# Outputs and maxima of an attention layer transposed on VectorE, outputs scaled on GpSimd, and a new order of the work

## The chip, the cores and the metric

The kernel runs on one core of a Trainium2 chip, as one launch. The metric is device time in microseconds (us), the median of three runs. The core's engines are TensorE (PE; PEld is its weight load), VectorE (DVE), ScalarE (ACT), GpSimd (POOL) and SyncE (SP), which here issues nearly all DMAs. Each engine works through its own instructions in order; semaphores tie them together.

## The reference

A layer over x of shape 4 x 1024 x 256 in float32: causal attention with 16 heads of 16 channels, a light feed-forward layer for all tokens, and a heavy one for 256 tokens of each batch, chosen by a router.

```python
xn = layernorm(x)
# attention; the reshape cuts the flat (token, channel) rows into 16 heads
qkv = (xn @ W_qkv + b_qkv).reshape(B, 16, S, -1)
q, k, v = split(qkv, 3, axis=-1)
qk = einsum('bhse,bhte->bhst', q, k) * 512 ** -0.5
attn = softmax(qk + causal_mask, axis=-1)
att = einsum('bhst,bhte->bhse', attn, v).reshape(B, S, -1) @ W_out + b_out
# feed-forward
light = gelu(rms_norm(xn, gamma_light) @ w1_light + b1_light) @ w2_light + b2_light
scores = coor_descent_route(xn, routing_token)      # 50 rounds of logsumexp
idx = top_k(scores, 256)
heavy = gelu(rms_norm(xn[idx], gamma_heavy) @ w1_heavy + b1_heavy) @ w2_heavy + b2_heavy
out = x + att + light + scatter(heavy, idx)
```

## The kernel before

**Front.** 32 tiles of 128 tokens are normalised, transposed on TensorE and projected to q, k, v and the routing score. VectorE adds the bias (`evacuate`, L1222) and SyncE stores each tile to DRAM (`qkv_d`, L612). Beside the last 16 tiles TensorE already does the transposes of q and k of the first steps and the maxima of step 0 (`FIRST`, `BESIDE`).

**Loop over 16 steps.** Step q holds four (batch, head) pairs, the "batches" c = 0 to 3. The work of a step:
- `T`: q and k are transposed (L968). ScalarE, VectorE (`R1`, L1244) and GpSimd (`SPLIT`, L1543, L1545) cut them into three bf16 pieces, which go through DRAM (`pieces_d`) into the operands `QTq` and `QTk`, rows 0 to 95. Operands have three buffers.
- `C`: 12 chunks of scores for each batch (L975), up to 512 columns wide, of which VectorE takes the row maxima only: L1256 where the chunk holds the diagonal (a custom instruction and one that reads its accumulator), L1259 where it doesn't. After chunk 11 of a batch a reduction gives the negated maxima `nm` (L1265).
- `MAX`: GpSimd cuts the maxima of one batch into three bf16 pieces (L1552 to L1557). `MT`: TensorE transposes them (L981), VectorE copies them (L1267), SyncE copies them into rows 96 to 98 of `QTq` (`load_m`, L658). They are subtracted inside the next matmul.
- `E`: 38 blocks of scores, keys on partitions (L1008), through two PSUM slots; ScalarE writes their exponentials to `strips` (L836). `CAUSAL`: GpSimd masks the diagonal (L1640).
- `PV`: 12 products with the values and a column of ones (L1026; four of 32 output rows side by side, two passes each, 8 matmul records), into `psO`.
- `OUT`: ScalarE copies the finished outputs to `osb` (L846). `OT`: TensorE transposes them in two halves (L987), and VectorE divides them by their sums (`normalise`, L1312 and L1317) into `pmo`. `SA`: one DMA stores them (L692).

`C` of a step runs about one step ahead of `E`. Router rounds (`R`, L1279, L1281, L1623) and a threshold search (`S`, L1286 to L1290) are mixed in. `T`, `C`, `MT` and `OT` share a ring of four PSUM slots (`MS`): TensorE waits until VectorE has freed the slot it needs (`free`). The order within each engine is made before the run by `schedule()`: it lets the engines advance in a model of costs (`TENSOR`, `VECTOR` and so on, `takes`), and picks, of what is ready, what is due first. The engines then run exactly this order. An item that isn't ready holds up all that stand behind it on its engine.

**After the loop** TensorE waits for the last output copy (`osb_done`) and does the light feed-forward layer (L1065) and the output projection in units; the last `OT` stands between the first two hidden products.

Two lines of `scores` and `product` matter for the waits:

```python
if kb == 0 and a == 0:
    pe.wait_ge(m_in[heads[0]], 16 * (q + 1))     # scores, one batch's maxima
...
if q > 0: pe.wait_ge(osb_done, q)                # product, kb == 0 and h == 0
```

## Time and profile before

| | us |
|---|---|
| median of three runs (792.14 to 795.06) | 793.27 |
| profiled execution | 791.96 |
| its span, first to last instruction | 790.2 |

| engine | busy us | share of the span |
|---|---|---|
| TensorE | 730.3 | 92% |
| VectorE | 576.0 | 73% |
| ScalarE | 435.3 | 55% |
| GpSimd | 366.9 | 46% |

Busy time is the time in which at least one instruction of the engine is under way. Matmuls are pipelined, so TensorE can be busy nearly all the time without being at its peak; the distance from one start to the next tells more than a duration. In the rows below `xN` is the number of instructions merged into a row, and "[t <-X]" says that the engine sat idle for t before the row, until X. The front takes some 130 us, the loop over steps 516, the rest 144.

### The profile page before, as it was taken

Reading aid. Unit: us, or ns where it says so; the run is one execution under the profiler, and the core shown is the slowest. Engines: PE = TensorE matmul, PEld = TensorE weight load, DVE = VectorE, ACT = ScalarE, POOL = GpSimd, SP = SyncE. Lnnn points to the kernel's source line nnn. Section 1 sums busy time; section 2 is a strip of 40 time slices with the busy share of each in tenths; the row PEclk is TensorE's granted clock in tenths of the full one; section 3 lists DMA queues with packets and bytes.
Section 4 is the critical chain, followed back from the end, with each engine's and each line's share of the span. In section 5 each row is a group of like instructions: output and inputs, shape, how many; then the busy total and the mean of one; then the engine's idle time right before and its main releaser. Section 6 shows DMA issues by size and latency. Waiting matters only on the chain.

```text
span 790.2 us, 13829 instructions
## 1 busy us (share of the span) xinstructions
PE 730.3 (92%) x4307; PEld 332.9 (42%) x4307; DVE 576.0 (73%) x1942; ACT 435.3 (55%) x940; POOL 366.9 (46%) x951
## 2 busy tenths in 40 slices
PE   5896998999899999999999999999999889978996
PEld 2563553333333333333333333333333238756655
DVE  4674776899899999999998999998998002554401
ACT  2232223577677777777777777767776661212240
POOL 5339102366565565755756556555332141235313
PEclk9999997799999999999999999999999999989999
DMA  9887854768989598678695795875902404652112
GB/s 286 212 203 164 210 160 111 150 120 96 194 116 102 113 98 125 116 76 147 98 108 108 90 140 103 88 129 62 129 7 29 121 7 131 197 174 93 11 17 27
DMA packets 246649, 92.18 MB, mean 117 GB/s; under 512 B 207504, under 2 KB 227120, under 8 KB 246576
## 3 DMA queue, kind: packets, MB, share of 16 engines
q1 hardware_dynamic: 245040, 89.20, 62.5%
q0 software_dynamic: 1536, 2.10, 1.7%
q8 instruction: 35, 0.57, 0.3%
q14 instruction: 38, 0.31, 0.2%
HBM read 56.26 MB, written 34.62 MB: 115 GB/s over the span
## 4 chain that ended last, share of the span: by engine, by line
PE 56%; DVE 29%; POOL 4%; issue 4%; ACT 3%; DMA 3%; SPq 1%; DVEq 0%; POOLq 0%
DVE ps L1256 12%; PE ps L1026 12%; PE ps L1008 10%; PE ps L975 9%; DVE mx L1259 8%; PE ps L943 7%; PE ps L1172 4%; PE ps L1185 3%; PE ps L1103 3%; ACT strips L836 2%; DVE mx L1256 2%; PE ps L1065 2%; PE ps L968 1%; PE ps L1099 1%; POOL roots L1499 1%
## 5 line engine op out<-in xcount | busy, mean ns | idle before, releaser
L836 ACT ACTIVATE strips<-ps 128x512 f32<-128x512 f32 (+1 forms) x608 | 325.9, 573 | 128.7 <-PE ps L1008 122.2
L1256 DVE CUSTOM_DVE_ANT_0 ps<-ps,maskrow 128x128 f32<-128x128 f32 (+3 forms) x512 | 244.7, 502 | 24.7 <-PE ps L975 23.9
L975 PE MATMUL ps<-QTk,QTq 96*128 96x512 bf16 (+3 forms) x768 | 212.9, 333 | 6.3 <-DVE mx L1256 2.7
L1008 PE MATMUL ps<-QTq,QTk 99*128 99x512 bf16 (+3 forms) x768 | 210.8, 334 | 7.3 <-ACT strips L836 4.2
L1259 DVE TENSOR_REDUCE mx<-ps 128x1 f32<-128x512 f32 x256 | 174.9, 683 | 16.2 <-PE ps L975 15.4
L1026 PE MATMUL ps<-strips,vext 128*32 128x512 f32 (+3 forms) x1536 | 165.0, 503 | 1.6 <-POOL strips L1640 1.1
L1008 PEld LDWEIGHTS ps<-QTq,QTk 99*128 99x128 bf16 x768 | 62.3, 97 | 142.3 <-ACT strips L836 115.8
L1640 POOL TENSOR_SCALAR_AFFINE_SELECT strips<-strips 128x512 f32<-128x512 f32 x128 | 80.4, 638 | 84.5 <-ACT strips L836 84.0
L975 PEld LDWEIGHTS ps<-QTk,QTq 96*128 96x128 bf16 x768 | 72.1, 98 | 112.3 <-DVE mx L1256 40.6
L943 PE MATMUL ps<-shared,xrT 128*128 128x384 f32 (+1 forms) x256 | 94.0, 502 | 1.2 <-DVE shared L1222 0.7
L1256 DVE DVE_READ_ACCUMULATOR2_ANT mx<- 128x1 f32 x512 | 71.6, 140 | 0.1
L943 PEld LDWEIGHTS ps<-shared,xrT 128*128 128x128 f32 x256 | 47.0, 195 | 30.7 <-issue 9.2
L1552 POOL CAST mW<-nm 128x8 bf16<-128x8 f32 x64 | 12.2, 190 | 100.6 <-DVE nm L1265 100.3
L1026 PEld LDWEIGHTS ps<-strips,vext 128*32 128x32 f32 x1536 | 30.7, 108 | 50.3 <-issue 39.8
L805 ACT ACTIVATE xrT<-ps 128x256 f32<-128x256 f32 x32 | 12.2, 380 | 54.8 <-PE ps L928 54.8
L1545 POOL TENSOR_TENSOR pieces<-r,pieces 128x512 bf16<-128x512 f32 x32 | 37.1, 1159 | 2.7
L1666 POOL TENSOR_TENSOR QTq<-QTq,shared 128x1024 f32<-128x1024 f32 x8 | 18.8, 2356 | 40.7 <-DMA QTq<-in_L_attn_inputs 40.6
L1392 DVE TENSOR_TENSOR QTk<-ps,QTq 128x256 f32<-128x256 f32 x32 | 13.4, 422 | 32.8 <-PE ps L1103 32.7
L791 ACT ACTIVATE xr<-strips,xshift,xscale 128x256 f32<-128x256 f32 x32 | 18.8, 592 | 28.8 <-POOLq L1515 28.8
L1103 PE MATMUL ps<-shared,strips 128*128 128x256 f32 x128 | 33.8, 388 | 0.0
L1312 DVE RECIPROCAL rden<-ps 128x16 f32<-128x16 f32 x32 | 7.9, 248 | 34.9 <-PE ps L987 34.9
L1543 POOL CAST pieces<-r 128x512 bf16<-128x512 f32 x32 | 19.5, 610 | 29.5 <-DVE r L1244 29.4
(153 smaller groups left out, 818.9 us busy)
## 6 DMA issues: line engine op xcount, KB each, us to landing
qkv_d<-shared SPq DMA_DIRECT2D x32, 384.0 KB, 3.1
pieces_d<-pieces SPq DMA_DIRECT2D x16, 768.0 KB, 3.4
QTq<-pieces_d SPq DMA_DIRECT2D x96, 128.0 KB, 4.2
QTk<-pieces_d SPq DMA_DIRECT2D x96, 128.0 KB, 6.7
qk<-qkv_d SPq DMA_DIRECT2D x64, 128.0 KB, 3.5
vext<-qkv_d SPq DMA_DIRECT2D x16, 256.0 KB, 8.7
sa_d<-pmo SPq DMA_DIRECT2D x16, 256.0 KB, 7.1
QTq<-sa_d SPq DMA_DIRECT2D x8, 512.0 KB, 5.8
```

The costliest lines, as they stand in the source:

```text
L836: nc.scalar.activation(dst, src, ACT.Exp, scale=SCALE).then_inc(exp_done, 1)
L943: mm = pe.matmul(psA[u][:, h, 0:n], transposed(t)[:, k, :], w_qkv[:, k, HW * h:HW * h + n], start=(k == 0), stop=(k == KE - 1))
L975: mm = pe.matmul(psM[:, s, 0:n], QTq[0:W, f % 3, c * 1024 + qb * P:c * 1024 + (qb + 1) * P], QTk[0:W, f % 3, c * 1024 + k0:c * 1024 + k0 + ...
L1008: mm = pe.matmul(psE[:, (NE * q + j) % ES, k * n:(k + 1) * n], QTk[0:W + 3, q % 3, c * 1024 + kb * P:c * 1024 + (kb + 1) * P], QTq[0:W + 3 ...
L1026: mm = pe.matmul(psO[32 * c:32 * c + 32, h, q0 - 512 * h:512], vext[:, u, 8 * c + kb, :], strip_at[kb][:, c, q0 - kb * P:q0 - kb * P + n], ...
L1103: mm = pe.matmul(o, saT[:, t % 2, k * P:(k + 1) * P], wout[:, k, :], start=False, stop=(k == KE - 1))
L1172: mm = pe.matmul(psO[:, m % 2, :], w1h[:, k, c * P:(c + 1) * P], xgT[:, k, h * 512:(h + 1) * 512], start=(k == 0), stop=(k == KE - 1))
L1185: mm = pe.matmul(o, hidT[:, c, st * P:(st + 1) * P], w2h[:, c, :], start=(c == 0), stop=(c == NHC - 1))
L1256: nc.vector.tensor_tensor_reduce(psM[:, s, 0:n], psM[:, s, 0:n], maskrow[:, 512 - n:512], 1.0, MASKED, ALU.add, ALU.max, acc).then_inc(fre ...
L1259: nc.vector.tensor_reduce(acc, psM[:, s, 0:n], AX.X, ALU.max).then_inc(free[s], 1)
L1545: pool.tensor_tensor(pieces[:, 2, halves], r1[:, h, :], pieces[:, 1, halves], ALU.subtract).then_inc(piece_done, 1)
L1640: pool.affine_select(out=diag, in_=diag, pattern=[[0, 4], [1, P]], compare_op=ALU.is_ge, fill=0.0, base=0, channel_multiplier=-1).then_inc ...
```

## The change

1. **Maxima.** `nm` now holds all four batches (128 x 32, one reduction a step), and VectorE transposes it in 32 x 32 blocks into `mxT` (`MXT`). GpSimd cuts it into pieces once a step. SyncE stores them with four DMAs to a DRAM tensor `m_d`, waits for the landing, and loads them with one DMA into rows 96 to 98 of `QTq`. The first exponent block of a step waits for this one load (`m_in`). For step 0 this stands behind the last store of the front. `MT`, the copy and the identity in bf16 are gone.
2. **Outputs.** VectorE transposes `psO` straight from PSUM, 128 x 512 at a time (`OT`), takes the reciprocals from the result (`OREC`), and GpSimd multiplies (`SA`). Four DMAs store a step's outputs where one did. ScalarE's copy and TensorE's transposes are gone. The ring carries `T` and `C` alone. A half of `psO` is free for the next step as soon as VectorE has transposed that half.
3. **Order.** The chunks of step 0 are spread over 13 tiles of the front, where it was 16. The costs in `schedule()` are new, a change between `PV` and other work on TensorE costs 0.1 in it, and so the order on every engine is another.

```diff
-FIRST = (... + [x for c in range(4) for x in
-            [("C", 0, c, k) for k in range(6)] + ([("MT", 0, c - 1)] if c else []) + ...
+FIRST = [("T", f, h) for f in range(2) for h in range(2)] + [("C", 0, c, k) for c in range(4) for k in range(12)]
...
-TENSOR = {"T": 0.95, "MT": 0.12, "OT": 0.95, "ST": 0.25}
+TENSOR = {"T": 0.55, "ST": 0.25}
-SYNC = {..., "LM": 0.5, "SA": 0.5, ...}
+SYNC = {..., "LM": 3.2, "SA": 2.0, ...}
...
             if kind == "E":
-                              done.get(("landed", ("LM", q, EXPS[j][1][0]))) if EXPS[j][0] == 0 else 0.0)
+                              done.get(("landed", ("LM", q))))
...
+    LAST_BESIDE = NT - 4
...
-            def load_m(f, c):
-                s, at = place["MT", f, c]
-                sp.wait_ge(free[s], at + 1)
-                sp.dma_start(QTq[W:W + 3, f % 3, c * 1024:(c + 1) * 1024].rearrange("i (n p) -> i n p", p=P),
-                             mT[:, c, :]).then_inc(m_in[c], 16)
+            def load_m(f):
+                sp.wait_ge(max_done, 4 * f + 4)
+                if f >= 3:
+                    sp.wait_ge(qk_ps, NE * (f - 2))
+                rows = m_d[f].rearrange("i (n g j) -> g n i j", g=4, j=32)
+                for g in range(4):
+                    sp.dma_start(rows[g], mP[32 * g:32 * g + 32, :, :]).then_inc(m_st, 16)
+                sp.wait_ge(m_st, 64 * (f + 1))
+                sp.dma_start(QTq[W:W + 3, f % 3, :], m_d[f]).then_inc(m_in, 16)
...
+                sp.wait_ge(sa_done, 2 * q + 2)
+                for c in range(4):
+                    sp.dma_start(sa_rows[q, c], pmo[32 * c:32 * c + 32, q % 2, :, :]).then_inc(sa_st[q % 2], 16)
...
-                nc.scalar.activation(osb[:, :], psO[:, :, :].rearrange("p h n -> p (h n)"), ACT.Copy).then_inc(osb_done, 1)
...
-                if kb == 0 and a == 0:
-                    pe.wait_ge(m_in[heads[0]], 16 * (q + 1))
+                if j == 0:
+                    pe.wait_ge(m_in, 16 * (q + 1))
...
-                if kb == 0 and h == 0:
+                if kb == 0:
                     pe.wait_ge(v_in[u], 16 * (q // 2 + 1))
                     if q > 0:
-                        pe.wait_ge(osb_done, q)
+                        pe.wait_ge(ot_done, 2 * (q - 1) + h + 1)
...
+            def largest_rows(f):
+                for k in (8, 9, 10, 11):
+                    s, at = place["C", f, 3, k]
+                    dve.wait_ge(free[s], at + 1)
+                if f > 0:
+                    dve.wait_ge(mxt_done, f)
+                nc.vector.tensor_reduce(nm[:, :], mx[:, f % 2, :, :], AX.X, ALU.max, negate=True).then_inc(nm_done, 1)
+                dve.wait_ge(nm_done, f + 1)
+                if f > 0:
+                    dve.wait_ge(max_done, 4 * f)
+                nc.vector.transpose(mxT[:, :], nm[:, :]).then_inc(mxt_done, 1)
+            def outputs(q, h):
+                dve.wait_ge(pv_done, NPV * q + (PVS_OF[3] - 1 if h == 0 else NPV))
+                if q > 0:
+                    dve.wait_ge(sa_done, 2 * (q - 1) + h + 1)
+                nc.vector.transpose(oT[:, h, :, :].rearrange("p b w -> p (b w)"), psO[:, h, :]).then_inc(ot_done, 1)
+            def denominators(q, h):
+                dve.wait_ge(ot_done, 2 * q + h + 1)
+                nc.vector.reciprocal(rden[:, h, :], oT[:, h, :, D]).then_inc(rden_done, 1)
...
+            def scaled(q, h):
+                pool.wait_ge(rden_done, 2 * q + h + 1)
+                if q >= 2:
+                    pool.wait_ge(sa_st[q % 2], 64 * (q // 2))
+                pool.tensor_tensor(pmo[:, q % 2, 16 * h:16 * h + 16, :], oT[:, h, :, 0:D],
+                                   rden[:, h, :].unsqueeze(2).to_broadcast([P, 16, D]), ALU.mult).then_inc(sa_done, 1)
```

**TensorE, where step 4's exponent blocks begin.** L1008 (before) and L982 (after) are exponent blocks, L975 and L960 chunks, L1026 and L1000 products. Before:

```order
L1008 MATMUL ps<-QTq,QTk 128x256
L1026 MATMUL ps<-strips,vext 32x512 [waits mask_done]
L1026 MATMUL ps<-strips,vext 32x512 x3
L1008 MATMUL ps<-QTq,QTk 128x128 [waits exp_done]
L1008 MATMUL ps<-QTq,QTk 128x128 x3
L975 MATMUL ps<-QTk,QTq 128x256 [waits free1]
L1008 MATMUL ps<-QTq,QTk 128x512 [waits m_in0,exp_done]
L975 MATMUL ps<-QTk,QTq 128x512 [waits free2]
L975 MATMUL ps<-QTk,QTq 128x384 [waits free3]
L975 MATMUL ps<-QTk,QTq 128x512 [waits free0]
```

And after:

```order
L960 MATMUL ps<-QTk,QTq 128x128 [waits free3]
L1000 MATMUL ps<-strips,vext 32x512 [waits mask_done]
L1000 MATMUL ps<-strips,vext 32x512 x3
L960 MATMUL ps<-QTk,QTq 128x256 [waits free0]
L960 MATMUL ps<-QTk,QTq 128x384 [waits free1]
L960 MATMUL ps<-QTk,QTq 128x512 [waits free2]
L960 MATMUL ps<-QTk,QTq 128x512 [waits free3]
L1000 MATMUL ps<-strips,vext 32x384 [waits mask_done]
L1000 MATMUL ps<-strips,vext 32x384 x3
L982 MATMUL ps<-QTq,QTk 128x512 [waits m_in,exp_done]
L982 MATMUL ps<-QTq,QTk 128x512 [waits exp_done]
```

The block that waits for maxima stood one chunk behind the last block of step 3. Now eleven chunks and two products stand between them, and 17 chunks between the last chunk of step 4 and that block, where it was 8.

**VectorE, where outputs are handled near the end of a step.** Before, the outputs come from the ring:

```order
L1256 ISA ps,mx<-ps,maskrow 128x512
L1256 ISA mx 128x1
L1265 TENSOR_REDUCE nm<-mx 128x8
L1312 RECIPROCAL rden<-ps 128x16
L1317 TENSOR_TENSOR pmo<-ps,rden 128x4x4x16
L1312 RECIPROCAL rden<-ps 128x16
L1317 TENSOR_TENSOR pmo<-ps,rden 128x4x4x16
L1256 ISA ps,mx<-ps,maskrow 128x128
```

And after, with the maxima of step 4 right behind:

```order
L1256 STREAM_TRANSPOSE oT<-ps 128x512
L1261 RECIPROCAL rden<-oT 128x16
L1228 ISA ps,mx<-ps,maskrow 128x512
L1228 ISA mx 128x1
L1269 STREAM_TRANSPOSE rT<-rsum 128x32
L1271 TENSOR_REDUCE zsum<-rT 128x1
L1243 TENSOR_REDUCE nm<-mx 128x32
L1248 STREAM_TRANSPOSE mxT<-nm 128x32
L1228 ISA ps,mx<-ps,maskrow 128x128
```

The multiplies are gone, a transpose of 512 columns stands ahead of each reciprocal, and the maximum is followed by its transpose.

**SyncE around the maxima.** L640 and L652 are the q/k pieces, L658 the copy of maxima before:

```order
L640 DMA pieces_d<-pieces 128x3072 [waits piece_done]
L658 DMA QTq<-mT 3x8x128 [waits free0]
L652 DMA QTq<-pieces_d 16x4x1024 [waits qk_ps,pieces_st]
L652 DMA QTq<-pieces_d 16x4x1024 x5
L652 DMA QTk<-pieces_d 16x4x1024 x6
L658 DMA QTq<-mT 3x8x128 [waits free0]
```

And after, where L661 and L663 are the stores and the load of maxima:

```order
L640 DMA pieces_d<-pieces 128x3072 [waits piece_done]
L661 DMA m_d<-mP 32x3x32 [waits qk_ps,max_done]
L661 DMA m_d<-mP 32x3x32 x3
L663 DMA QTq<-m_d 3x4096 [waits m_st]
L652 DMA QTq<-pieces_d 16x4x1024 [waits qk_ps,pieces_st]
L652 DMA QTq<-pieces_d 16x4x1024 x5
```

Five DMAs with a wait between them stand where four single copies were spread over the step.

## Rows read from the trace of the kernel before

**Rows 1.** Stretch, length, busy us of PE, PEld, DVE, ACT, POOL; clock, DMA, GB/s.
```profile
166.60:609.90 443.30, 429.22 (x2942) 157.64 (x2935) 412.42 (x1457) 320.62 (x707) 243.95 (x699) 1.00 0.74 105
```

**Rows 2.** VectorE in time, ends of steps 1 and 15: start, duration, instruction, [idle before].
```profile
166.63 0.17 DVE L1265 TENSOR_REDUCE nm<-mx 128x8 f32<-128x16 f32 x1
...
609.53 0.14 DVE L1256 DVE_READ_ACCUMULATOR2_ANT mx<- 128x1 f32 x1
609.81 0.17 DVE L1265 TENSOR_REDUCE nm<-mx 128x8 f32<-128x16 f32 x1
```

**Rows 3.** VectorE groups in the loop: xcount | busy us, mean ns | idle before, releasers.
```profile
L1256 DVE CUSTOM_DVE_ANT_0 ps<-ps,maskrow 128x128 f32<-128x128 f32 x448 | 213.8, 503 | 10.5 <-PE ps L975 9.7 <-DVE nm L1265 0.3
L1259 DVE TENSOR_REDUCE mx<-ps 128x1 f32<-128x512 f32 x224 | 153.0, 683 | 7.5 <-PE ps L975 6.8
...
L1267 DVE COPY mT<-ps 24x128 bf16<-24x128 bf16 x56 | 11.5, 205 | 1.3 <-PE ps L981 1.2
L1265 DVE TENSOR_REDUCE nm<-mx 128x8 f32<-128x16 f32 x57 | 9.7, 170 | 7.8
L1279 DVE STREAM_TRANSPOSE rT<-rsum 128x32 f32<-128x32 f32 x48 | 9.6, 201 | 0.0
...
L1288 DVE STREAM_TRANSPOSE countT<-counted 128x96 f32<-128x96 f32 x16 | 4.5, 279 | 0.5
```

**Rows 4.** TensorE in time, around 301 us.
```profile
300.96 1.06 PE L1026 MATMUL ps<-strips,vext 128*32 128x512 f32 x8
301.96 0.60 PE L1008 MATMUL ps<-QTq,QTk 99*128 99x512 bf16 x2
302.40 0.65 PE L975 MATMUL ps<-QTk,QTq 96*128 96x256 bf16 x3
```

**Rows 5.** TensorE in time in the tail, and the group of output copies.
```profile
614.46 0.63 PE L1008 MATMUL ps<-QTq,QTk 99*128 99x128 bf16 x5
...
647.84 1.04 PE L987 MATMUL ps<-ident,osb 128*128 128x128 f32 x8
648.71 1.88 PE L1065 MATMUL ps<-xrT,w1l 128*128 128x512 f32 x4
...
L846 ACT ACTIVATE osb<-ps 128x1024 f32<-128x1024 f32 x16 | 16.4, 1024 | 3.0 <-PE ps L1026 2.7
```

**Rows 6.** VectorE in time, around 310 us.
```profile
309.06 0.25 DVE L1312 RECIPROCAL rden<-ps 128x16 f32<-128x16 f32 x1
309.34 0.42 DVE L1317 TENSOR_TENSOR pmo<-ps,rden 128x256 f32<-128x256 f32 x1
309.68 0.25 DVE L1312 RECIPROCAL rden<-ps 128x16 f32<-128x16 f32 x1
...
311.53 0.17 DVE L1265 TENSOR_REDUCE nm<-mx 128x8 f32<-128x16 f32 x1
311.67 0.30 DVE L1256 CUSTOM_DVE_ANT_0 ps<-ps,maskrow 128x128 f32<-128x128 f32 x1
```

**Rows 7.** GpSimd groups in the loop.
```profile
L1545 POOL TENSOR_TENSOR pieces<-r,pieces 128x512 bf16<-128x512 f32 x24 | 27.8, 1159 | 2.0
...
L1554 POOL TENSOR_TENSOR mW<-nm,mW 128x8 bf16<-128x8 f32 x56 | 11.3, 202 | 4.8
```

**Rows 8.** DMA issues (KB each, median us to landing), then SyncE in time.
```profile
s_d<-sT SPq DMA_DIRECT2D x1, 16.0 KB, 3.1
rs<-s_d SPq DMA_DIRECT2D x1, 16.0 KB, 1.7
...
na_all<-na_d SPq DMA_DIRECT2D x1, 4.0 KB, 3.7
...
128.08 0.72 SPq L658 DMA_DIRECT2D QTq<-mT  x1
...
142.91 1.97 SPq L706 DMA_DIRECT2D osb<-s_d  x4
```

**Rows 9.** TensorE in time, where the loop over steps starts.
```profile
130.39 1.97 PE L968 MATMUL ps<-ident,qk 128*128 128x128 f32 x8 [2.64 <-DVE shared L1222]
```

More of the change, by code:

```diff
@@ L212, in ready @@
             if kind == "MAX":
-                return after(("Vector", ("C", x[1], x[2], 11)))
+                return latest(after(("Vector", ("MXT", x[1]))), done.get(("landed", ("LM", x[1] - 1))))
             if kind == "CAUSAL":
@@ L219, in ready @@
                 return after(("Vector", x))
+            if kind == "SA":
+                return latest(after(("Vector", ("OREC",) + x[1:])), 0.0 if x[1] < 2 else done.get(("landed", ("SA", x[1] - 2))))
             return after(("Vector", ("SMAX",)))
@@ L296, in schedule @@
         start = max(start, ready(engine, x))
+        if engine == "Tensor" and order[engine] and (x[0] == "PV") != (order[engine][-1][0] == "PV"):
+            start += 0.1
         end = start + takes(engine, x)
@@ L1607, in _ @@
                 split(1, h)
-            for c in range(3):
-                maxima(0, c)
+            maxima(0)
             def route_z(r):
```

214 lines of the change are left out of this document (85 added, 129 removed).

## The prediction

> **What bounds the kernel now.** I first looked at the busy time of each engine in stretches, then at its groups of instructions there, then at single instructions in order of time. The stretch that matters lies between the last maximum of step 1 (166.63) and that of step 15 (609.81) [rows 2]: 443.2 us for 14 steps, **31.66 us a step**, at the full granted clock of 2.4 GHz [rows 1]. In it VectorE (DVE) is busy 412.4 of 443.3 us, 93%; what its own idle time waits for is chunks of TensorE's line L975 [rows 3]. TensorE shows 429.2 us, 97%, but its matmuls overlap: the successor of a product of 1.06 starts 1.00 after it, and that of two 512-column matmuls of 0.60 together 0.44 after them [rows 4]. So TensorE has to be counted by starts: score matmuls cost 0.22 per 512 columns, and a step has 36 + 36 such widths (15.8 us), 12 products (nine full widths at 1.0 and some entry cost, 9.4), 8 transposes of q and k (about 0.9), 8 of outputs (0.87, 647.84 to 648.71 [rows 5]) and 4 of maxima (some 0.15 each, a guess from the 0.11 of an output's, 0.6). That is 27.6 of 31.66, 87%. So VectorE is nearer to its limit, and TensorE close behind; both take from the four-slot ring, each in a fixed order.
>
> VectorE too must be read by starts: the multiply of 0.42 starts 0.34 before the next instruction, so about 0.08 of each duration is overlapped [rows 6].
>
> **VectorE, per step.** Removed: four times the wait before the maximum over a batch (609.53 to 609.81, 0.28 [rows 2]) and the maximum (311.53 to 311.67, 0.14 [rows 6]), 1.68; four copies of transposed maxima, 205 ns less the overlap [rows 3], 0.52; twice reciprocal and multiply, 0.28 + 0.34 [rows 6], 1.24. Sum 3.44.
> Added: one wait of 0.28; one maximum from 64 elements, 170 ns for 16 [rows 3] with some 0.9 ns for each more, 0.21; the transpose behind it, which waits for its end (0.03, as the multiply does) and costs 201 ns less overlap, together 0.66. Output transposes of 128x512 out of PSUM aren't in the trace. From below, a reduction of the same 512 PSUM columns takes 683 ns; from above, 201 ns for 32 columns and 279 for 96 [rows 3] give 1.22 ns a column, 786 ns for 512. I take 0.70, nearer to the row that reads the same tile. With 0.03 of wait and a reciprocal of 0.17 that is 0.90 a half, 1.80 a step. Sum 2.46. **Net -0.98 a step, -13.7 us over 14** (-11.3 to -14.2 by the two ends).
> The Trainium skill (Vector Engine (DVE) Microarchitecture Reference, 3.8 The reshape front-end and per-opcode configuration) has the transpose sustain one element per cycle per lane. By it the lower end holds, and the sum would be 0.5 us better.
>
> **TensorE, ScalarE, GpSimd.** TensorE loses 0.87 + 0.6 = 1.5 a step and six of 54 ring entries; ScalarE loses one copy of 1024 ns [rows 5]; GpSimd loses sixteen 0.2 us pieces and gains four and two multiplies of half the 1159 ns row [rows 7]. None of these sets the period alone. But VectorE's waits for L975 are 9.7 + 6.8 = 16.5 us [rows 3], and less load and fewer ring entries ahead must shorten them. Bounds 0 and -16.5; I take a third, **-6**.
>
> **The new path of the maxima.** Before, the first exponent block of a step needed one batch's maxima. Now it needs all four, last chunk of the step included, and behind it on TensorE, in order, stand the chunks that feed VectorE. The chain, from the last chunk's end:
> - VectorE 0.28 + 0.21 + 0.03 + 0.20 = 0.72
> - GpSimd, four pieces: 202 ns at 8 wide, 1159 at 512 [rows 7], so 0.25 at 32 wide; with gaps 1.1, and 0.4 until it is free (0 to 1.2)
> - SyncE: four stores. Four loads in a row took 1.97 to issue, one copy of maxima 0.72 [rows 8]; the last store starts 1.5 in (1.2 to 2.2)
> - its landing, 3.1 as the one small store to DRAM; then the load, 1.7 and 3.7 as two small loads [rows 8], taken 2.1, nearer to the one that reads plain rows
> - handovers from engine to engine, some 0.3.
>
> **Sum 9.2 us**, ends 8.0 and 12.4.
>
> The Trainium skill (DMA: Bandwidth & Descriptors, Anatomy of one DMA) puts a fixed cost of about 2.0 us on each DMA, most of it the receipt of the write, which speaks against a detour through DRAM. The trace's store is dearer, 3.1 [rows 8]. By the page's figure the two transfers would be 4.0 instead of 5.2 and the chain 8.0, an estimate; the forecast would then be the case "the chain fits" below.
>
> Cover: TensorE must have filled VectorE until then. In TensorE's order of step 4, 17 chunks stand between the last chunk and the block that waits, against 8 before; the exponent blocks of step 3 are all done eleven chunks before it. A batch of 12 costs VectorE 8 x 0.42 + 4 x 0.60 = 5.8 less overlap [rows 3]; counted so, with the transposes and routing work among them, the cover of steps 1 to 14 is 7.8 to 12.1, mean 9.2. VectorE runs again 0.4 after the landing, at 9.6. The shortfalls sum to 12.5 us; part falls where VectorE idled anyway (2.2 a step, 443.3 less 412.4 over 14), 3.5 off: **+9**.
>
> SyncE is blocked some 4 us more a step; behind it stand the twelve loads of q/k pieces that TensorE needs a step later, so nothing, as long as they have that step. The four stores of outputs in place of one carry the same packets: nothing, at most their issues.
>
> **The ends.** Start: TensorE idles 2.64 us before 130.39 because VectorE has chunks to reduce between the last projections [rows 9]; these now end three tiles earlier, -1.5. But the load of step 0's maxima is issued behind the last qkv store, which waits for the same evacuation as TensorE at 130.39: 1.5 + 3.1 + 2.1 puts the first exponent block near 137, where it now follows the transposes at 132.4 [rows 9]. Three chunks stand ahead of it, 1 us of VectorE's work: +3.3; step 1 keeps its -1.0. Sum +0.8. Tail: VectorE's last chunk ends at 609.5 [rows 2], step 15's first block is the fifth matmul of the row at 614.46, about 614.9 [rows 5], 5.4 later; now 9.3, +3.9. Both remaining 1.0 us copies on ScalarE go from the path, and the transposes between the first two hidden products (0.87) [rows 5]: -2.9. Sum +1.0.
>
> **Sum**: -13.7 - 6 + 9 + 0.8 + 1.0 = -8.9. The profiled execution took 791.96 (span 790.2 and 1.8 around it): 783.1. The median, 793.27, is 1.3 above it, so 784.4, **forecast 784.5 us**.
>
> **Rivals.**
> *The maxima come too late (slower).* Place: the first exponent block of each step. Every us of chain beyond 9.6 less cover is lost once a step, some 15 us in all; the sum crosses zero at a chain of 9.8, only 0.6 above mine. With issues as the copies of maxima have today (2.2 for three) and the load 0.5 later it is 10.4: +9, 802. With the 3.7 us load too it is over 815. For it: that load [rows 8], and that three of the four links of the chain are queues with other work. Against: nothing is issued while SyncE waits, so the load finds the queue empty.
> *The chain fits.* At 8.4 or less the shortfalls nearly vanish: -17 to -20, 773.
> *The gain is given back by density (same).* Exponent blocks and products held back by the wait crowd into the remaining 20 us or so: some 30 of 38 blocks, 34 chunks and 7 of 12 products, 18.6 us of TensorE by the prices above, 93%, with ScalarE's two slots to be refilled in turn. If that keeps VectorE's idle time as it is and adds a little, -6 falls away and +2 comes: 792.
> *The transposes aren't what they seem*: at 1.0 us each the net on VectorE halves, +8, 792 too.
>
> **Chances.** Forecast case (776 to 789) 0.42; fits (below 776) 0.15; given back (789 to 797) 0.18; late maxima (above 797) 0.25. 0.5% is about 4 us, about what a measurement tells from no change; so faster by more 0.57, within it 0.18, slower 0.25. The range is **768 to 806**: it takes in a chain from 8.0 to some 10.7 and leaves out the worst landings.
>
> **What would show it.** The distance from a step's last chunk to its first exponent block: 9.2, and TensorE waiting for the DMA of QTq there 1 to 3 us in most steps. VectorE's output transpose near 0.70, and its work a step lower by 1. Step length: 31.0. Tail from last chunk to first hidden product some 34.5, now 36.5. If the landing of a small store plus load is above 6 us, the forecast is wrong on the slow side; if TensorE hardly waits for QTq, on the fast side; if it hardly waits and the step is still 31.7, the bound was TensorE's order and not VectorE's work.

## The result, and the profile after

The changed kernel took **802.1 us** (median of four runs, 798.3 to 804.5), 1.011 times the time of before, 95% interval 1.0077 to 1.0145. Twelve more runs beside others of before gave 798.4 (795.1 to 804.3), ratio 1.0068 [1.0041, 1.0094]. So it is slower by 5 to 9 us, where 784.5 and faster was forecast; 802 lies in the range of 768 to 806. The profiled execution took 799.7, span 797.8.

The span falls into four parts. The first ends with the end of VectorE's last chunk of step 1, the second (14 steps) with that of step 15, the third with TensorE's last product, the fourth is what follows the loop. Profiled spans, us:

| kernel | start | loop | a step | tail | behind | span | median, ratio to before |
|---|---|---|---|---|---|---|---|
| before | 166.4 | 443.2 | 31.66 | 35.3 | 145.4 | 790.2 | 1 |
| changed | 168.2 | 442.6 | 31.61 | 37.6 | 149.4 | 797.8 | 802.1, 1.011 |
| changed, again | 166.6 | 445.5 | 31.82 | 37.0 | 146.8 | 795.9 | 798.4, 1.007 |
| costs_only | 170.3 | 436.8 | 31.20 | 33.2 | 144.8 | 785.1 | 786.8, 0.992 |
| outputs_only | 170.5 | 455.7 | 32.55 | 30.4 | 149.1 | 805.7 | 807.0, 1.017 |
| maxima_only | 167.6 | 438.7 | 31.34 | 34.8 | 143.8 | 784.9 | 788.1, 0.993 |

The loop, forecast to gain 10.7, gained 0.6. The start lost 1.8, the tail 2.4, what follows the loop 4.0.

The answer to [rows 1] in the changed kernel (length, then busy us of PE, PEld, DVE, ACT, POOL, the granted clock, the DMA share, GB/s):

```profile
168.20:610.80 442.60, 419.39 (x2756) 146.17 (x2756) 404.94 (x1372) 303.62 (x694) 231.67 (x560) 0.97 0.74 105
```

VectorE is busy 404.9 us instead of 412.4: the work did leave it. Its groups in the same stretch, the answer to [rows 3] (xcount | busy, mean ns | idle before, releasers):

```profile
L1228 DVE CUSTOM_DVE_ANT_0 ps<-ps,maskrow 128x512 f32<-128x512 f32 x449 | 212.9, 506 | 13.9 <-PE ps L960 13.3
L1231 DVE TENSOR_REDUCE mx<-ps 128x1 f32<-128x512 f32 x224 | 153.4, 685 | 14.8 <-PE ps L960 14.6
...
L1256 DVE STREAM_TRANSPOSE oT<-ps 128x512 f32<-128x512 f32 x27 | 19.2, 712 | 1.8 <-PE ps L1000 1.4
```

The chunks cost what they did (506 and 685 ns, 503 and 683 before). The new transpose of the outputs costs 712 ns, the forecast's 0.70. But VectorE now waits 13.3 + 14.6 = **27.9 us** for TensorE's chunks, 16.5 before, and its idle time as a whole rose from 30.9 to 37.7. That is where the gain went. Nearly all of this waiting, 25.2 us of it (15.9 before), falls between a step's first exponent block and the next step's last chunk.

What TensorE's own idle time in the loop waited for (releaser: us, times, longest):

```profile
PE ps L960 <- DVE mx L1231: 5.1, 16, 0.7
PE ps L960 <- DVE mx L1228: 4.8, 16, 0.5
PE ps L982 <- DMA QTq<-m_d: 4.4, 5, 2.3
PE ps L982 <- ACT strips L833: 3.7, 15, 0.4
```

In five of the 14 steps it stood idle for the load of maxima, 4.4 us in all, and half of that in step 2. There (start, duration, [idle before, releaser]):

```profile
209.27 0.39 PE L960 MATMUL ps<-QTk,QTq 96*128 96x512 bf16 x1
211.92 0.59 PE L982 MATMUL ps<-QTq,QTk 99*128 99x512 bf16 x2 [2.26 <-DMA QTq<-m_d]
```

and what SyncE issued ahead of those maxima (L715 is the first of seven weight loads, L661 the four stores of maxima, L663 the load):

```profile
197.93 0.38 SPq L715 DMA_DIRECT2D shared<-in_L_ffn_w_light  x1
...
202.30 1.85 SPq L661 DMA_DIRECT2D m_d<-mP  x4
209.16 0.25 SPq L663 DMA_DIRECT2D QTq<-m_d  x1
```

The maxima of step 2 were ready by 202, and the stores stood behind the weight loads: the last landed 5 us after its issue, and the load could go at 209.16 only. The step's chain, here from the end of its last chunk on VectorE to the end of the first matmul of its first exponent block, was 12.6 us. In step 11 it was 12.4, with 22 chunks in TensorE's order ahead of the block; over the other steps 7.3 to 9.9; the mean of steps 1 to 15 is 8.9.

### The profile page after: what moved, and what is told of

It reads as the page before. It is cut to its first block, busy times and chain, and to the rows that moved or that the text cites. A ratio compares the mean times of both kernels' runs of the same rounds, so it can differ in the third digit from the quotient of the medians.

```text
span 797.8 us, 13083 instructions
## 1 busy us (share of the span) xinstructions
PE 722.7 (91%) x4115; PEld 322.8 (40%) x4115; DVE 568.7 (71%) x1846; ACT 417.2 (52%) x924; POOL 352.3 (44%) x790
## 4 chain that ended last, share of the span: by engine, by line
PE 59%; DVE 15%; DMA 9%; POOL 7%; ACT 4%; issue 3%; SPq 2%; DVEq 0%; POOLq 0%
PE ps L1000 14%; PE ps L982 13%; PE ps L960 11%; PE ps L928 6%; DVE ps L1228 5%; DVE mx L1231 4%; PE ps L1144 4%; ACT strips L833 3%; PE ps L1157 3%; DMA QTq<-sa_d 2%; DMA QTq<-m_d 2%; PE ps L1075 2%; DMA m_d<-mP 2%; POOL roots L1484 1%; PE ps L953 1%
## 5 line engine op out<-in xcount | busy, mean ns | idle before, releaser
L982 PE MATMUL ps<-QTq,QTk 99*128 99x512 bf16 (+3 forms) x768 | 214.0, 341 | 20.2 <-DMA QTq<-m_d 8.7
L960 PE MATMUL ps<-QTk,QTq 96*128 96x512 bf16 (+3 forms) x768 | 215.7, 339 | 16.4 <-DVE mx L1228 7.1
L1000 PE MATMUL ps<-strips,vext 128*32 128x512 f32 (+3 forms) x1536 | 166.4, 510 | 0.9 <-POOL strips L1634 0.8
L982 PEld LDWEIGHTS ps<-QTq,QTk 99*128 99x128 bf16 x768 | 62.1, 98 | 181.2 <-ACT strips L833 145.4
L960 PEld LDWEIGHTS ps<-QTk,QTq 96*128 96x128 bf16 x768 | 74.1, 99 | 125.9 <-DVE mx L1228 39.2
L928 PE MATMUL ps<-shared,xrT 128*128 128x384 f32 (+1 forms) x256 | 96.1, 514 | 0.0
L928 PEld LDWEIGHTS ps<-shared,xrT 128*128 128x128 f32 x256 | 49.0, 202 | 28.8 <-issue 7.8
L1000 PEld LDWEIGHTS ps<-strips,vext 128*32 128x32 f32 x1536 | 31.3, 109 | 50.2 <-issue 41.7
L1256 DVE STREAM_TRANSPOSE oT<-ps 128x512 f32<-128x512 f32 x32 | 22.8, 712 | 35.7 <-PE ps L1000 35.3
L802 ACT ACTIVATE xrT<-ps 128x256 f32<-128x256 f32 x32 | 12.2, 381 | 58.8 <-PE ps L913 58.7
L1551 POOL TENSOR_TENSOR pmo<-oT,rden 128x256 f32<-128x256 f32 x32 | 19.8, 619 | 43.6 <-DVE rden L1261 43.4
L1378 DVE TENSOR_TENSOR QTk<-ps,QTq 128x256 f32<-128x256 f32 x32 | 13.3, 422 | 35.0 <-PE ps L1075 34.9
L1075 PE MATMUL ps<-shared,strips 128*128 128x256 f32 x128 | 34.8, 396 | 0.0
L870 ACT ACTIVATE strips<-ps 128x256 f32<-128x256 f32 x32 | 12.1, 382 | 42.3 <-PE ps L1059 42.3
```

Of the source, the lines that this page charges most:

```text
L928: mm = pe.matmul(psA[u][:, h, 0:n], transposed(t)[:, k, :], w_qkv[:, k, HW * h:HW * h + n], start=(k == 0), stop=(k == KE - 1))
L960: mm = pe.matmul(psM[:, s, 0:n], QTq[0:W, f % 3, c * 1024 + qb * P:c * 1024 + (qb + 1) * P], QTk[0:W, f % 3, c * 1024 + k0:c * 1024 + k0 + ...
L982: mm = pe.matmul(psE[:, (NE * q + j) % ES, k * n:(k + 1) * n], QTk[0:W + 3, q % 3, c * 1024 + kb * P:c * 1024 + (kb + 1) * P], QTq[0:W + 3 ...
L1000: mm = pe.matmul(psO[32 * c:32 * c + 32, h, q0 - 512 * h:512], vext[:, u, 8 * c + kb, :], strip_at[kb][:, c, q0 - kb * P:q0 - kb * P + n], ...
L1075: mm = pe.matmul(o, saT[:, t % 2, k * P:(k + 1) * P], wout[:, k, :], start=False, stop=(k == KE - 1))
```

## The experiments

All are timed against before on the same chip and given as ratios; differences between the tables' medians include the chip's share, some 2 us.

### Which part costs what

The change has three parts that can be had apart: the table of costs from which the order is made, the path of the outputs, and the path of the maxima.

```
# costs_only = before with
-    return max(0.13, n / 2400 + 0.01)
+    return 0.00042 * n + 0.005
# and the like for transposes, chunks and products; a change between products and other work costs 0.1
# outputs_only = costs_only + the new path of the outputs (maxima batch by batch, as before)
# maxima_only  = the changed kernel with the outputs' old path (copy on ScalarE, transposes on TensorE)
```

> The kernel before with nothing but the new table of costs for products, chunks and transposes, from which the order is made anew. If VectorE's work sets the step, the order hardly matters: 790 to 795 us, steps of 31.5 to 31.8. If the new order itself is what costs the changed kernel its gain (exponent blocks crowded, the ring filled later), the loss shows here without either new path: 798 or more.

> The outputs by the new path (transposed by VectorE out of PSUM, scaled by GpSimd), the maxima batch by batch as before, new costs. By the prediction's prices VectorE pays 1.80 instead of 1.24 a step (+7.8 us over 14), TensorE's 8 transposes and the two 1.0 us copies go (-4 of waiting, -2.9 at the tail): 790 to 796, and TensorE at the full clock from 147 us to the end of the loop, since no block waits for a whole step's maxima. If instead the new outputs are what lost the time: 798 or more, with half-clock stretches in the loop.

> The maxima once a step through DRAM, the outputs as before, new costs. By the prediction's prices -1.54 a step on VectorE (-21.6), +9 for late maxima, +4.7 at start and tail: 785 without any clock term. If TensorE's clock halves behind the waits for the maxima, as in the changed kernel, some 6 to 10 us more, 791 to 795, with half-clock stretches near steps 0, 2 and 11 again. If the maxima alone account for the whole loss: above 798.

Measured: costs_only 786.8, ratio 0.992 [0.989, 0.996]. outputs_only **807.0**, 1.017 [1.011, 1.023]. maxima_only 788.1, 0.993 [0.990, 0.996], and once more beside the changed kernel 786.2, 0.990 [0.987, 0.994]. VectorE's waits in the loops of costs_only and of maxima_only (engine, line, releaser: us, times, longest):

```profile
DVE mx L1261 <- PE ps L977: 6.3, 14, 0.9
DVE ps L1258 <- PE ps L977: 4.1, 11, 0.6
```

```profile
DVE ps L1251 <- PE ps L975: 18.8, 35, 1.8
DVE mx L1254 <- PE ps L975: 10.2, 18, 1.7
```

I had expected the order to matter little. **The new order alone is worth 6 us**: with the same work as before, VectorE waits 10.4 us for chunks instead of 16.5. The maxima's new path takes 11.7 us of work from VectorE in the loop (399.5 busy against 411.2) and raises the waiting for chunks from 10.4 to 29.0: +18.6. Its idle time as a whole rises by 13.6, from 25.6 to 39.2, since it has fewer short gaps between instructions. Work and idle time cancel, and it comes out no faster than costs_only. The outputs' new path costs 20 us on top of costs_only.

### The place of a small load in a queue

In outputs_only TensorE stood idle five times for the fourth batch's maxima. In step 4, 2.90 us long (the longest, in step 10, is 3.89): what SyncE issued, and TensorE in the same stretch:

```profile
270.53 2.68 SPq L658 DMA_DIRECT2D QTq<-pieces_d  x6
273.25 0.90 SPq L658 DMA_DIRECT2D QTk<-pieces_d  x2
274.19 0.74 SPq L664 DMA_DIRECT2D QTq<-mT  x1
```

```profile
277.64 0.23 PE L970 MATMUL ps<-identb,mW 128*24 128x128 bf16 x1
280.76 1.01 PE L991 MATMUL ps<-QTq,QTk 99*128 99x512 bf16 x2 [2.90 <-DMA QTq<-mT]
```

The maxima were in place at 273.4. Their load of 6 KB stood behind eight piece loads of 128 KB and landed 5.7 us after its issue, where the median of such loads is 1.5. In costs_only's order the same load stands ahead of the piece loads in all steps but one.

```
# outputs_ahead = outputs_only with, at the end of schedule():
+    for f in (1, 2, 3, 4, 7, 9, 10):
+        line.remove(("LM", f, 3))
+        line.insert(line.index(("BULK",) if f == 2 else ("LOAD", f + 2, 0)), ("LM", f, 3))
# sync_order = the changed kernel with
+    line.remove(("BULK",)); line.insert(line.index(("LOAD", 4, 2)) + 1, ("BULK",))
+    line.remove(("LM", 11)); line.insert(line.index(("LOAD", 13, 0)), ("LM", 11))
```

> outputs_only with the load of the fourth batch's maxima moved ahead of the piece loads (in step 2 of the weight loads) in SyncE's order, in the seven steps where the new order had put it behind one or two groups of them; in costs_only, 20 us faster, it stands ahead of them in all but step 1. If that place in the queue is what cost the 20 us (TensorE idle for the maxima, then the half clock): no idle time of TensorE above 1 us in the loop, full clock, and the 0.6 us a step of VectorE's added work remain over costs_only: 793 to 797. If the new path of the outputs costs by itself: 803 to 807.

> The changed kernel with two items moved in SyncE's order: the seven large weight loads go from just ahead of step 2's maxima to behind the last piece load of the next step, and step 11's maxima go ahead of a group of piece loads. The two long chains (12.6 and 12.4 us) fall to 8 or 9. If those two and the half clock behind them are a good part of the loss: 36.6 to about 32 for step 3, 1 us at steps 12 and 13, 795 to 797 in all. If the loss lies in every step: 800 to 802.

Measured: outputs_ahead 795.9, 1.0045 [1.0017, 1.0073], against 1.017: **0.012 of the 0.024 that separate outputs_only from costs_only are the load's place**. Not all went as expected: the weight loads, now behind the maxima's load, held up a group of piece loads, TensorE idled 3.35 us for those, and the granted clock stood at half for 20 us of the loop. Of the other half, against costs_only's profile, 5.0 us are more work of VectorE in the loop (416.2 against 411.2), 4.6 more idle time of it there, and 3.6 stand behind the loop. sync_order 797.2, 1.0029 [0.9999, 1.0059], against 1.0068 to 1.011; this interval and that of the twelve runs (from 1.0041) overlap, so a gain of the whole kernel is likely but not shown. Its runs spread from 788.6 to 799.6, and the profile is of the fastest, so of it I use only the steps: the interval to step 3's last chunk fell from 36.6 to 31.8, as forecast. Step 11's chain stayed at 12.4: that one was not SyncE's place but TensorE's own order, 7 us of it at half clock in both kernels (489.4 to 496.2 in the changed one).

```profile
197.50:229.30 31.80, 30.07 (x208) 10.09 (x207) 28.96 (x100) 22.28 (x53) 17.02 (x41) 1.00 0.79 150
```

### The clock, or the wait itself

Behind several of these idle stretches the granted clock stood at half (1.2 GHz) for 3 to 10 us: from 171.9, 212.9, 489.4 and 557.6 in the loop of the changed kernel, from 619 in the tail; in before there was no such stretch between 147 and 628. To tell the clock's share from the wait's, TensorE was given matmuls that nobody reads while it would wait: in filled 125 of them by the trace (110 were planned), ahead of the blocks that wait and behind the chunks before them; in outputs_filled 49.

```
# filled = the changed kernel, TensorE's loop with (n and the places left out here)
+                pe.wait_ge(exp_done, NE * q)
+                for k in range(n):
+                    pe.matmul(psE[:, 0, :], QTk[0:W, q % 3, 0:P], QTq[0:W, q % 3, 0:512], start=True, stop=True)
# outputs_filled = outputs_only, ahead of the wait for a batch's maxima
+            FILL = {(2, 0): 0, (2, 6): 6, (3, 6): 7, (4, 6): 13, (9, 6): 6, (10, 6): 17}
```

> The changed kernel with 110 more 128x512 matmuls on TensorE whose results nobody reads: one behind each chunk between a step's last chunk and its first exponent block (once the blocks of the step before are done), and 12, 10, 4, 4 and 6 directly ahead of the block that waits, in steps 0, 2, 11, 13 and 15. Nothing that the kernel waits for comes earlier. If the clock that halves behind TensorE's idle time is what costs, the half-clock stretches at 213 to 223, 489 to 496 and 558 to 564 us go, the interval to step 3's last chunk falls from 36.6 to about 32, and the time falls from 802 to 793 to 797 although TensorE has more to do. If the clock is a bystander and the late maxima themselves cost: 802 or up to 8 us more.

> outputs_only (807) with 6, 7, 13, 6 and 17 idle-time matmuls of 128x512 ahead of the blocks on which TensorE stood idle 1.3 to 3.9 us for a batch's maxima (the seventh block of steps 2, 3, 4, 9 and 10). If its loss of 20 us against costs_only is mostly the half clock behind these five waits: the half-clock stretches from 245 to 487 us go and the time falls to 790 to 796. If the loss is VectorE's and GpSimd's added work: 805 to 810.

Measured: filled 799.4, 1.0073 [1.0034, 1.0112]; outputs_filled 797.2, 1.0044 [1.0013, 1.0075]. Step 2 to 3 in the changed kernel and in filled, then step 4 to 5 in outputs_only and in outputs_filled:

```profile
199.80:236.40 36.60, 33.75 (x207) 11.37 (x204) 29.76 (x99) 22.77 (x53) 17.15 (x41) 0.86 0.83 147
```

```profile
197.00:233.30 36.30, 34.51 (x228) 12.10 (x227) 29.67 (x100) 22.28 (x53) 16.98 (x41) 1.00 0.85 134
```

```profile
269.60:305.40 35.80, 31.56 (x187) 10.59 (x183) 29.06 (x103) 20.00 (x46) 19.10 (x54) 0.86 0.63 75
```

```profile
262.80:295.30 32.50, 30.80 (x196) 10.99 (x196) 28.64 (x103) 19.66 (x45) 19.10 (x54) 1.00 0.72 82
```

In filled the clock went from 0.86 to 1.00 and the step stayed at 36.3, against the expectation of 32. The step has to be cut in two to see why. From the first exponent block to the next last chunk it took 21.3 us instead of 24.0, so the half clock had cost **2.7 us** there; but the chain ahead of it had grown from 12.6 to 15.0, since ten extra matmuls ran until 211.6 while the load had landed at 209.7. The same in step 13: 23.6 to 21.3, 2.3 for the clock. In outputs_only, where the counts fitted the waits, the gain shows: 1.0167 to 1.0044, some 10 us (8.3 of them in the loops of the two profiles), with 34 us of half clock gone (from 245, 279, 443, 480 and 549) and 3.5 come in (from 368.5). The waits that outputs_ahead shortens are the same ones, and it stands at the same 1.0045: the two gains are not shown to add. So the clock is a real part, 2.3 to 2.7 us for the two stretches of 7 and 10 us that could be priced; in the changed kernel it explains some 5 us of the loop and 3 of the tail, not the whole loss. What the stretch in step 11's chain cost is not shown, since filled has matmuls of its own there (12.6 against 12.4).

Cut in two like this, the steps show a thing that the prediction had missed. Last chunk to first block ("chain"), and from there to the next last chunk ("rest"), us. The four kernels have the same order on TensorE; in step 2 the changed kernel and pieces3, in step 13 the changed kernel, hold 7 to 10 us of half clock in the rest:

| step | changed | filled | sync_order | pieces3 |
|---|---|---|---|---|
| 2 | 12.6 + 24.0 | 15.0 + 21.3 | 10.2 + 21.7 | 13.7 + 24.0 |
| 5 | 7.9 + 22.4 | 9.3 + 22.4 | 7.9 + 22.4 | 7.9 + 22.4 |
| 8 | 8.3 + 22.2 | 8.0 + 22.2 | 8.4 + 22.2 | 7.6 + 22.4 |
| 10 | 8.1 + 25.0 | 9.3 + 25.0 | 8.2 + 25.0 | 8.0 + 25.0 |
| 11 | 12.4 + 21.1 | 12.6 + 21.1 | 12.4 + 21.1 | 11.4 + 21.1 |
| 13 | 8.2 + 23.6 | 7.9 + 21.3 | 7.7 + 21.3 | 7.4 + 21.5 |

**At the full clock the rest of a step is the same to 0.4 us in each of the four, however long the chain ahead of it was.** (In combined, below, the rest of step 10 holds 13.6 us of half clock and takes 29.5 instead of 25.0.) Nothing of a late chain is caught up within the step: TensorE's order behind the first block is a fixed string of blocks, products and chunks, and it takes 20 to 25 us in each step, 22.7 on average in the changed kernel with the half clock in it; in before it is 27.7. In these stretches of the changed kernel TensorE is busy 97% of the time, VectorE 91% and ScalarE 79% (before: 97, 93 and 73).

### A shorter chain

```
# pieces3 = the changed kernel, load_m: three stores of 128 partitions, each as its piece is there
-                sp.wait_ge(max_done, 4 * f + 4)
...
-                for g in range(4):
-                    sp.dma_start(rows[g], mP[32 * g:32 * g + 32, :, :]).then_inc(m_st, 16)
+                for i, ready in enumerate((1, 2, 4)):
+                    sp.wait_ge(max_done, 4 * f + ready)
+                    sp.dma_start(rows[i], mP[:, i, :]).then_inc(m_st, 16)
...
# maxima_pieces = maxima_only with the same
```

> The changed kernel, but the maxima go out by piece (3 stores of 128 partitions, each as soon as its piece is there) instead of 4 stores of 32 partitions behind the last piece: the chain from a step's last chunk to its first exponent block gets about 1 us shorter, 9.0 to 8.0 on average. If the lateness of the maxima and the clock that halves behind it are what was lost: 793 to 799 against 802. If the chain is covered in most steps and only the two long ones (12.6 and 12.4, which stand behind other loads) cost anything: 800 to 802.

> maxima_only with the stores by piece. The chain gets 1 us shorter (9.0 to 8.0). If lateness is paid in every step: -5 or more, 780 to 783. If only a few uncovered steps pay: 785 to 788.

Measured: pieces3 792.1, 0.9999 [0.9976, 1.0022]; maxima_pieces 784.2, 0.989 [0.986, 0.991]. By the ratios pieces3 is 5 to 9 us better than the changed kernel, as the "lateness" side expected, but not for its reason: the mean chain fell by 0.2 us only (8.9 to 8.8). The load landed 0.5 us earlier on average, but only in steps 2 and 10 did TensorE still stand idle for it; elsewhere the chunks that the order places ahead of the first block took that long. Of pieces3's gain 4.3 us is the tail (37.6 to 33.3: the last chain 8.8 to 7.3, and no half clock behind it), 3.1 the loop. maxima_pieces is 1 to 4 us better than maxima_only (0.993 and 0.990); its interval overlaps both of theirs, so that gain is not shown.

### Maxima twice a step

If the first block could come earlier in the order, VectorE's and TensorE's work would overlap again. The maxima of batches 0 to 2 are sent as soon as the third batch is reduced, those of batch 3 at the end; the seventh block of a step is the first to need the latter.

```
# maxima_twice = maxima_pieces with ("MXT", f, p), ("MAX", f, p), ("LM", f, p), p in (0, 1); in schedule():
-                              done.get(("landed", ("LM", q))))
+                              done.get(("landed", ("LM", q, 0 if j < 6 else 1))))
# after_twice = pieces3 with the same
```

> maxima_pieces, but the maxima go twice a step: those of batches 0 to 2 as soon as the third batch is reduced, those of batch 3 at the step's end (two maxima and transposes on VectorE, eight pieces on GpSimd, six stores and two loads). VectorE has 0.5 to 0.66 us a step more to do, +7 to +9 over 14 steps. If the step's gain was given back because all 38 exponent blocks are squeezed in behind the late maxima, and VectorE then starves for chunks (28 us of waiting in maxima_only, 10 in costs_only): its waiting falls to 10 to 15 us and the time to 778 to 784. If VectorE's work decides: 5 to 9 us above maxima_pieces.

> The changed kernel with stores by piece and maxima sent twice a step (batches 0 to 2, then batch 3). Against pieces3, 792, VectorE has 0.5 to 0.66 us a step more to do. If VectorE's starvation behind the late, crowded exponent blocks is what ate the gain in the changed kernel too: its waiting for chunks falls from 25 us to 10 to 15 and the time to 784 to 788. If the new outputs hold the step back by themselves: 791 or more.

Measured: maxima_twice **780.6**, 0.984 [0.982, 0.987]; after_twice 785.5, 0.989 [0.981, 0.998]. The loop of maxima_twice and VectorE's waits in it (the first and the fourth are for chunks):

```profile
167.70:601.00 433.30, 417.43 (x2873) 156.09 (x2865) 400.88 (x1401) 318.19 (x710) 227.49 (x590) 0.99 0.81 110
```

```profile
DVE ps L1257 <- PE ps L980: 7.3, 14, 1.4
DVE nm L1276 <- DVE mx L1257: 6.5, 28, 0.2
DVE rden L1286 <- PE ps L987: 5.8, 3, 5.1
DVE mx L1260 <- PE ps L980: 5.3, 14, 0.9
```

VectorE has 1.5 us more to do than in maxima_pieces (400.9 against 399.4) and waits 12.6 us for chunks instead of 27.3. Its loop is 3.6 us shorter (436.9 to 433.3), less than the 14.7 us of waiting that went: 3.5 us more are spent waiting for its own last maxima, and 5.8 for transposed outputs, 5.1 of it once, of which twice_bulk (below) has 1.3 left and a loop of 431.3. So that VectorE starves for chunks because the exponent blocks come late and crowded is **shown** in the old outputs' path, by waits and a time that came as expected; it is worth 4 to 6 us of the loop there, not the whole 14.7, and the planner's order changed with it. In the new path the waiting falls likewise (25.2 to 16.3), VectorE's work grows by 3.7, the loop falls by 2.1 only, and the time by 1%, with intervals that touch.

### Behind the loop

```
# route_early: the wait and the product behind GpSimd's loop over its order go,
-            pool.wait_ge(th, search_steps(ROUNDS) - 4)
-            pool.tensor_scalar(route[:, 1:2], found[:, :].bitcast(F32), sign[:, :], None, ALU.mult).then_inc(th, 1)
# and the product comes into the loop
                elif item[0] == "S":
                    search(item[1])
+                    if item[1] == ROUNDS - 1:
+                        pool.tensor_scalar(route[:, 1:2], found[:, :].bitcast(F32), sign[:, :], None, ALU.mult).then_inc(th, 1)
# costs_route = costs_only with the same; combined = the changed kernel with route_early, sync_order and pieces3
```

> The changed kernel with nothing but GpSimd's product for the router's second number moved from behind the last scaling to behind the search. In the changed kernel the store of that number waited for it until 650.57 (644.75 before) and VectorE then 7.8 us for its landing. If the 4 us lost behind the loop (149.4 against 145.3) are this wait: 798 to 799. If combined's 142.5 came from the clock and the other moves: 801 to 802.

> costs_only with the router's second number done right behind the search. There the two small transfers were not held up by a scaling, so little is left to gain: 785 to 787. If the 7 us that combined gained behind the loop come from this product alone and not from the clock: 780 to 783.

> The changed kernel with three things moved and nothing computed otherwise: the maxima stored by piece (as in pieces3, 792), the two moves of sync_order, and GpSimd's product for the router's second number done right behind the search and not behind the last scaling of the outputs, where the two small transfers and VectorE's first step of the choice waited for it 7.8 us. By the theory (chain and clock): step 3 falls to 32, -5; -3 to -4 after the loop: 783 to 786. If the 150.7 us after the loop don't move by the early product: 788. If the sync moves bring nothing beyond pieces3: 790.

In the changed kernel GpSimd's last scaling comes between the last mask and the router's product, and SyncE waits for that product:

```profile
649.59 0.62 POOL L1551 TENSOR_TENSOR pmo<-oT,rden 128x256 f32<-128x256 f32 x1 [1.64 <-DVE rden L1261]
650.20 0.30 POOL L1656 TENSOR_SCALAR route<-found,sign 128x1 f32<-128x1 f32 x1
```

```profile
650.57 0.34 SPq L756 DMA_DIRECT2D na_d<-route  x1
653.80 0.36 SPq L758 DMA_DIRECT2D na_all<-na_d  x1
```

VectorE's wait for it, in the changed kernel and (1.4 us) in before:

```profile
DVE kth L1342 <- DMA na_all<-na_d: 7.8, 1, 7.8
```

```profile
DVE kth L1356 <- DMA na_all<-na_d: 1.4, 1, 1.4
```

Measured: route_early 792.9, 0.9993 [0.9962, 1.0025]; the part behind the loop 143.0 us instead of 149.4 (146.8 in the changed kernel's second profile), and no such wait is left. I had expected 798 to 799, a gain of 3 to 4 us; it is 4 to 6 by this part of the profiles, and 6 by the ratio to that of the twelve runs. costs_route 786.5, 0.990 [0.987, 0.994] against 0.992: nothing to tell, where no scaling stood ahead. combined **785.0**, 0.988 [0.984, 0.991], as expected: a few moved lines turn the changed kernel from slower into faster than before.

### What the outputs' path costs when the rest is mended

```
# twice_bulk = maxima_twice with the weight loads behind ("LOAD", 4, 2) and the product early
# after_twice_bulk = after_twice with the same two: the changed kernel with every mend
```

> maxima_twice (780.6; old path of the outputs) with the seven weight loads moved behind step 4's piece loads and the router's product early. In maxima_twice step 2's fourth batch of maxima still landed behind the weight loads: TensorE stood idle 4.67 us and the interval to step 3's last chunk was 36.0. By chain and clock 4 to 5 us go: 775 to 777. If the weight loads merely collide with something else there: 779 to 781.

> twice_bulk with the new path of the outputs, that is the changed kernel with every mend. By VectorE's work alone, 1.80 against 1.24 us a step, it stands 6 to 8 us above twice_bulk, 782 to 785; if what TensorE and ScalarE are spared by the new path makes up for that: 774 to 778; if the new outputs also cost through queues: 787 or more.

> The changed kernel itself once more, in more runs, since route_early (792.9) came out 9 us below its first four runs (802.1) where its profile shows 6.4 us less behind the loop and 3.4 less ahead of it, which that edit cannot touch. If the 802 stands on other chips: 800 to 803. If those four runs were high by the 3 us that the front part varies: 797 to 800.

> maxima_only once more, beside the changed kernel on one chip, to take their difference (the new path of the outputs, with the late maxima) without a change of chip: 14 us by the first runs; 8 to 10 if the changed kernel's first runs were high. By route_early 6.4 of it is the wait behind the loop.

Measured on one chip: twice_bulk 780.7, 0.986 [0.980, 0.991]; after_twice_bulk 780.2, 0.983 [0.977, 0.989]. So twice_bulk brought nothing over maxima_twice (780.6), where 4 to 5 us were expected: the wait moved from step 2 to step 3, TensorE idle 2.24 us at 239.98, and while the loop is 2.0 us shorter, the tail is 1.6 longer. And the outputs' new path costs **nothing that can be told** once chain and queues are mended, with four runs each and intervals of some 0.6% to either side: its loop is 10.7 us longer in the profiles (442.0 against 431.3), but that profile is of its slowest run and has 27 us of half clock in the loop where the other has 3, and its tail (29.5 against 34.8) and the part behind the loop (143.3 against 145.1) are shorter. In the changed kernel as it is, the same path costs 12.2 us (798.4 against 786.2): 5.8 in the loop, 2.2 in the tail and 1.8 behind it in the two profiles of that chip, 9.9 in all.

Three kernels stand at 780 to 781, some 12 us below before; between them these runs don't decide.

## Why the prediction was wrong, point by point

**VectorE's work, -0.98 a step: right.** Busy time per step fell from 29.45 to 28.92 (412.4 and 404.9 over 14), and the wait ahead of the maximum, 7.8 us in [rows 3], is 2.1: 0.53 + 0.41 = 0.94. The transposes took 712 ns (0.70 forecast; the reduction that I took as the nearest row has 683). The rival "1.0 us each" is out. By the Trainium skill's rule (Vector Engine (DVE) Microarchitecture Reference, 3.8) the prediction had the lower end of 683 hold; the trace is 29 ns above it.

**"Less waiting behind TensorE, -6": the step that failed.** Its reasoning was that less load on TensorE must shorten VectorE's waits. They went from 16.5 up to 27.9. The curious thing is that 6.1 us of shorter waiting did exist, but from the new order alone (costs_only 10.4), which the prediction did not cost at all since nothing is added or removed by it; that its size is that of the forecast term is chance.

**"Late maxima, +9": mis-sized, and by a wrong rule.** The distance from last chunk to first block was forecast at 9.2 and measured at 8.9, but that it fits is in part luck: the load itself had landed 8.1 us behind the last chunk on average, 7.5 without the two long chains. A wait of TensorE for it of 1 to 3 us was forecast for most steps; it had one in five of 14 steps, 0.2 to 0.7 us and once 2.3, and the step was still 31.6. The prediction had named this as the sign that "the bound was TensorE's order and not VectorE's work", and this is what came. What was wrong is the price. The prediction charged only the part of the chain that was not covered by chunks. The cover kept VectorE busy during the chain, but TensorE then has nearly the same exponent blocks to do in 22.7 us instead of 27.7 (36 of a step's 48 exponent matmuls start there, 38 before) and cannot hurry (the "rest" above), and VectorE starves there: 25.2 of its 27.9 us of waiting lie in the rest, 2.7 in the chains. That is +17.5 against costs_only's 10.4, some of it from the half clock, where +9 stood in the sum.

So the loop's sum should have read -13.2 (work) + 11.4 (waiting, 16.5 to 27.9) = -1.8; measured was -0.6.

**The rivals.** "Given back by density" names this mechanism, the blocks and products crowded into the rest of the step; its price was +2 on VectorE's waiting where 11.4 came, and its chance 0.18. "Too late" forecast the right time, 802, for another reason: its chain of 10.4 did not come. Only steps 2 and 11 were that late. That the measured time lies so near to it, and within the range, is luck.

**"Nothing" for SyncE: wrong.** The prediction wrote that behind a blocked SyncE only the piece loads wait. It looked at what waits behind the maxima and not at what the new order puts ahead of them: seven weight loads in step 2. In outputs_only the new order put the fourth load of maxima behind the piece loads; that the outputs' four stores, at 2.0 in the table of costs where one had 0.5, pushed it there is argued, not shown.

**Start and tail, +0.8 and +1.0.** Start 1.8 (0.2 in the second profile; among five kernels that have the front part alike it ends between 164.8 and 168.2, so this can't be told). Tail 2.4, 1.0 forecast: the two terms came, the last chain was 8.8 (9.3), and the half clock from 619 to 629 was missing from the sum. Last chunk to first hidden product: 37.6, forecast 34.5.

**Behind the loop, 0: wrong, 1.4 to 4.** The moved step was the scaling, from VectorE to GpSimd, and it had a wait; what was queued behind that wait on GpSimd was the router's product, and behind that two transfers and VectorE's choice of tokens.

**The clock** stood in no term. The prediction had TensorE waiting 1 to 3 us for the load in most steps and did not ask what its clock would do behind such a wait: 1.2 GHz for some us behind those of step 2 and of the tail.

## What to carry to other kernels

An order written by a planner is a change of its own: run it alone first. A transfer that comes later is not paid by its uncovered part only; ask how long the work behind it takes at the least, and whether the engine that has to do it was already nearly full. And when a wait is put on an engine or a transfer on a queue, read both what stands behind it and what stands ahead of it: here three small moves (combined) were worth 15 to 19 us.

## What the runs showed of the hardware that I had not expected

- A 6 KB load issued behind eight of 128 KB on the same queue landed 5.7 us after the end of its issue, against 1.5 in the median, and the stores of maxima behind the weight loads 5.0 to 5.7, against 1.1. A small transfer's landing here is that of what was issued just ahead of it: the load landed at 280.6 and the last piece load ahead of it at 280.8, the first store at 208.4 and the last weight load at 208.4. Without such a backlog a store of maxima took 1.5 from the start of its issue and the load 2.5, together 4.0, where the prediction had 5.2 by the same measure. The Trainium skill (DMA: Bandwidth & Descriptors, Anatomy of one DMA) has a fixed cost of about 2.0 us for each DMA, for those that GpSimd issues; these are SyncE's. The sum agrees, the store alone is cheaper, the load dearer, and the queued ones are far above it.
- TensorE's granted clock fell to half, 1.2 GHz, behind idle times of 1.29 us (at 619.05, half from 619 to 629), 1.44 and 2.26 us, and not behind one of 1.31 (outputs_only, 209.57); and it also stood at half from 489.4 in the changed kernel, where no single idle time just before was above 0.4 us but chunks came at VectorE's pace. With the waits filled by unread matmuls it stayed at 2.4 GHz throughout the loop in filled, and but for 3.5 us in outputs_filled. The Trainium skill (TensorE: Matmul & The Clock Gate, HAM oscillation) tells of kernels whose clock halves behind waits for DMAs; this trace agrees.
- Runs of one kernel can spread by 11 us (sync_order, 788.6 to 799.6; after_twice, 777.6 to 789.0), where another's lie within 1.3 (maxima_pieces, 783.8 to 785.0). What sets that stays open.
